# Weight loads moved from ScalarE's queue into SP's queue of x, one group ahead, in a ten-table embedding kernel

## The reference

```
embs    = [x_i @ w_i for i in 0..9]                 # x_i: 1024 x vocab_i, w_i: vocab_i x 64, float32
emb_sum = sum(embs)
q_emb   = sum((x_i ** 2) @ (w_i ** 2))
out     = concatenate([0.5 * (emb_sum ** 2 - q_emb)] + embs, axis=-1)
```

## Time and profile before

| | |
|---|---|
| median of 3 runs | 277.24 us (277.16 to 277.35) |
| profiled execution | 277.28 us |
| its span | 275.5 us |
| busy in the span | PE 214.9, DVE 222.2, ACT 225.6, POOL 117.5 us |
| moved by DMA | 113.92 MB, mean 413 GB/s |

### The profile page before, as it was taken

One profiled execution on the slowest core, in us unless ns is written; L12 is line 12 of the kernel. 1 busy time (PEld: TensorE's weight loads), 2 busy tenths in 40 slices (PEclk: granted clock), 3 DMA queues, 4 the chain that ended last, 5 costly groups with the idle time before them and its releaser, 6 DMA issues.

```text
span 275.5 us, 2719 instructions
## 1 busy us (share of the span) xinstructions
PE 214.9 (78%) x894; PEld 151.5 (55%) x894; DVE 222.2 (81%) x132; ACT 225.6 (82%) x272; POOL 117.5 (43%) x83
## 2 busy tenths in 40 slices
PE   0529889799988777878886887787688788698995
PEld 0416566576756555556664654554555555466752
DVE  2776876888798898878978978978987987999973
ACT  0648998999987788889868868868877887899984
POOL 0446667685414109257224134134045041083934
PEclk9977999999999999999999999999999999999999
DMA  7999999999999999999999999999999999999996
GB/s 257 436 412 431 419 424 414 427 425 426 421 425 425 421 426 421 422 426 427 421 432 422 426 423 424 423 426 430 418 426 428 421 431 425 407 420 415 410 396 231
DMA packets 15710, 113.92 MB, mean 413 GB/s; under 512 B 2000, under 2 KB 3280, under 8 KB 9168
## 3 DMA queue, kind: packets, MB, share of 16 engines
q1 hardware_dynamic: 11088, 106.96, 92.6%
q10 hardware_dynamic: 4608, 6.79, 6.7%
HBM read 110.85 MB, written 2.88 MB: 413 GB/s over the span
## 4 chain that ended last, share of the span: by engine, by line
DMA 71%; issue 13%; ACT 10%; PE 3%; POOLq 1%; POOL 1%; ACTq 1%; DVE 0%; SPq 0%
DMA x_ring<-in_x_dram 62%; DMA whole<-in_w_dram 8%; ACT is_set L380 7%; PE sums L518 2%; ACT turned L391 1%; ACT whole L372 1%; POOLq L197 1%; POOL is_one L498 1%; ACT results L396 1%; ACT L372 0%; ACTq L366 0%; ACT turned L440 0%; PE sums L573 0%; DVE is_one L614 0%; ACT odd_flag L443 0%
## 5 line engine op out<-in xcount | busy, mean ns | idle before, releaser
L614 DVE TENSOR_SCALAR_CACHE_REDUCE is_one<-x_ring 128x4096 uint8<-128x4096 f32 (+2 forms) x58 | 218.4, 3776 | 45.7 <-DMA x_ring<-in_x_dram 44.5
L380 ACT ACTIVATE is_set<-x_ring 128x2048 fp32r<-128x2048 uint32 (+2 forms) x106 | 190.1, 1796 | 32.1 <-DMA x_ring<-in_x_dram 31.7
L518 PE MATMUL sums<-is_set,low 128*128 128x512 f32 x396 | 133.0, 417 | 57.2 <-ACT is_set L380 42.5
L518 PE MATMUL sums<-is_set,high 128*128 128x512 f32 x396 | 125.2, 397 | 0.0
L518 PEld LDWEIGHTS sums<-is_set,low 128*128 128x128 f32 x396 | 68.3, 191 | 97.4 <-ACT is_set L380 42.7
L474 POOL CAST high<-whole 128x1024 fp32r<-128x1024 f32 (+5 forms) x31 | 27.1, 875 | 141.1 <-ACT whole L372 141.1
L518 PEld LDWEIGHTS sums<-is_set,high 128*128 128x128 f32 x396 | 75.5, 191 | 17.4
L476 POOL TENSOR_TENSOR low<-whole,high 128x1024 fp32r<-128x1024 f32 (+5 forms) x31 | 60.8, 1960 | 2.5
L372 ACT ACTIVATE whole<-whole 128x512 f32<-128x512 f32 (+5 forms) x31 | 16.5, 536 | 7.0 <-DMA whole<-in_w_dram 6.9
L380 ACT ACTIVATION_READ_ACCUMULATOR is_set<-x_ring 128x1 f32 x106 | 19.8, 186 | 0.0
L487 POOL TENSOR_TENSOR total<-total,turned 128x1024 f32<-128x1024 f32 x8 | 19.2, 2399 | 0.0
(11 more groups left out here) (38 smaller groups left out, 14.7 us busy)
## 6 DMA issues: line engine op xcount, KB each, us to landing
x_ring<-in_x_dram SPq DMA_DIRECT2D x42, 2048.0 KB, 21.3
x_ring<-in_x_dram SPq DMA_DIRECT2D x9, 1024.0 KB, 19.1
x_ring<-in_x_dram SPq DMA_DIRECT2D x11, 512.0 KB, 17.8
whole<-in_w_dram ACTq DMA_DIRECT2D x21, 256.0 KB, 9.7
out_dram<-results SPq DMA_DIRECT2D x9, 256.0 KB, 9.1
x_ring<-in_x_dram SPq DMA_DIRECT2D x4, 256.0 KB, 14.3
whole<-in_w_dram ACTq DMA_DIRECT2D x2, 192.0 KB, 7.2
whole<-in_w_dram ACTq DMA_DIRECT2D x4, 64.0 KB, 8.8
```

The source lines that it names most:

```text
L380: nc.scalar.activation(is_set[chunk.k % SETS][:, 0:length], in_ring(chunk.place, length).bitcast(U32), ACT.Sign, accum_out=set_counts[:, c ...
L518: last = nc.tensor.matmul(sums[:, summing(n, half), :], w, x[:, at:at + HALF], start=first, stop=False, skip_group_check=True)
L614: nc.vector.tensor_scalar(is_one[c % 2][:, 0:length], in_ring(at, length), 1.0, None, ALU.is_equal, ALU.add, accum_out=one_counts[:, c:c + ...
```

## The change

`AHEAD` becomes 2, and ScalarE issues no weights. SP does it between its loads of x: x load 0, then the weights of groups 0, 1 and 2, x load 1, and from there on the weights of group g+1 ahead of the first load of x of group g. The wait for `parts_ready` goes with them into SP's queue. `AHEAD` also sets when ScalarE squares (group g+1 after the third chunk of group g, where it was g+2) and when GpSimd adds a table's sums (one group after the copy, where it was two).

```
-AHEAD = 3
+AHEAD = 2
@@ plan_counts
         for load in own:
-            load.count = counts[-1]
+            load.count, load.group = counts[-1], one.group
@@ block.sync
-            free = 0
+            def load_w(group):
+                if group.g >= WHOLES:
+                    sp.wait_ge(parts_ready, group.g - WHOLES + 1)
+                at, n = group.tile * D, group.tiles
+                sp.dma_start(whole[group.whole][:, 0, 0:n, :], w_dram[group.table][:, at:at + n * D]
+                             ).then_inc(w_landed[group.whole], 16)
+
+            free, fetched = 0, 1
             for load in LOADS:
+                if load.i == 1:
+                    load_w(GROUPS[0])
+                while load.i > 0 and fetched < min(load.group.g + AHEAD, NGROUPS):
+                    load_w(GROUPS[fetched])
+                    fetched += 1
                 if load.free > free:
@@ block.scalar
-            def load_w(group):
...
-            for group in GROUPS[:AHEAD]:
-                load_w(group)
             act.wait_ge(constants, 8)
             for group in GROUPS[:AHEAD - 1]:
                 square(group)
             for group in GROUPS:
                 for c, chunk in enumerate(group.chunks):
                     count_set(chunk)
-                    if c == min(1, len(group.chunks) - 1):
-                        if group.g + AHEAD < NGROUPS:
-                            load_w(GROUPS[group.g + AHEAD])
                     if c == min(2, len(group.chunks) - 1) and group.g + AHEAD - 1 < NGROUPS:
                         square(GROUPS[group.g + AHEAD - 1])
```

## The result

| | before | after |
|---|---|---|
| median of 6 runs | 277.24 us (277.1 to 277.35) | 284.12 us (281.29 to 284.79) |
| ratio | | 1.0227 (95% interval 1.019 to 1.0264) |
| profiled execution, span | 277.28, 275.5 us | 284.56, 282.8 us |
| busy PE, DVE, ACT, POOL | 214.9, 222.2, 225.6, 117.5 us | 217.6, 222.5, 226.3, 117.5 us |

The kernel is slower, as forecast, but by 6.9 us where 3.9 were forecast, and the time lies outside the range of 279.9 to 283.0 us. Its runs also scatter over 3.5 us, where those of the kernel before agree within 0.25.

The account below looks back on a forecast made before the run. The prediction took the DMA stream of x plus a fixed tail to bound the kernel. Its terms, 0 + 0 + 3.9 + 0 + 0, on 277.24 gave 281.1 us, with a range of 279.9 to 283.0 us.

Parts of the forecast that it names:

- a stream and a fixed tail: Whole kernel: x in transfer without a hole until 267.0 us, then some 6.7 us of small work on the last tile.
- SP's added issues: SP's queue: 31 more issues, 10 to 14 us against 210 us of waiting, counted at 0.
- ScalarE's freed ones: ScalarE: 31 issues, 10.4 us, go; nothing waits for its queue while the stream is full, counted at 0.
- The first wait: Start of SP's queue: the weights of group 3 wait for group 0's split, with x behind; a hole of 3.9 us.
- The end: Last group squared after chunk 97 instead of 93; weighing ends 0.7 us before GpSimd's last masks, so hidden, counted at 0.
- The wait of w8: SP's queue: group 8's weights hold back x load 9 until group 5 is split; margin -0.2 to +1.2 us, counted 0.
- a second hole at w8: Rival: group 5 ready 1 to 3 us later adds 0.5 to 2.5 us, 281.6 to 283.6; 0.22 together with the end.
- No change: Rival: who issues makes no difference, if group 3's weights find x still in transfer; 277.2 us, chance 0.03.
- faster: Rival: one queue runs the DMA engines better than two in turns, at 436 GB/s some 276.2 us; chance 0.05.

Follow-up runs that it names:

- e6: Changed kernel with five buffers of weights instead of three and three of parts instead of four, same order in SP's queue; 277.07 us.
- e12: Changed kernel run a third time as it is, for its spread; 281.93 us, ratio 1.0155 to the kernel before.
- e0: Changed kernel run again as it is, for a trace with another time; 281.71 us, ratio 1.0149 to the kernel before.
- e3: Changed kernel with only the square of group 5 moved, to after chunk 5 as in the kernel before; 281.01 us.
- e5: Changed kernel with the product of the low part left out in chunks 3 to 7 (tables 4 and 7); 281.74 us.
- e8: Changed kernel with each product of chunks 3 to 7 (tables 4 and 7) made twice; 286.10 us.
- e1: Changed kernel with ScalarE issuing the weights of groups 3 to 5 where the kernel before did, SP all others; 278.60 us.
- e9: Changed kernel with the weights of group g+1 behind the last load of x of group g, except the last three groups; 277.22 us.

## Why the prediction was wrong

**What held.** That the kernel is a stream and a fixed tail: the tail stayed at 6.7 us, and spans differ by their holes and by the lag of the last part, a term that the prediction did not have. SP's added issues cost nothing and ScalarE's freed ones gave nothing that shows (e6 has both and full slices; its 0.5 us under the kernel before has no cause shown). The first wait: 3.9 us forecast, 3.8 to 4.0 us in every trace of the changed kernel. Here two small misses cancelled. w3 was issued at 8.97 us and not at 9.28, but the stream ran again in effect from 10.66 us, worked out from the 568 KB of the stretch 10 to 12 us at 425 GB/s. That is 1.7 us after the issue, where 1.4 was taken between bounds of 1.0 and 1.9. The first packet of w3 started 0.95 us after its issue. The Trainium skill's 0.6 us to the first byte ("DMA: Bandwidth & Descriptors", Specifications), by which the prediction made the hole 3.1 us, is shorter than the trace's time; the hole of 3.8 us goes with the trace. The end was covered, as worked out: the weighing ends at 272.8 us, the masks start at 273.9. The lowest run of each of the three sets, 281.13 to 281.29 us, is the forecast of 281.1, one hole and no more.

**The step that failed** is "The wait of w8", counted at 0: "ScalarE needed from 22.08 us (chunk 3) to 35.2 us (end of chunk 7), 13.1 us almost without a gap", so it "can start there. Chunk 7 ends at 32.7 us". I took a stretch in which ScalarE was busy for one in which ScalarE alone sets the pace. Before, TensorE did chunk 3 and what follows at the high clock. In the profile after it did chunks 3 and 4 at 1.2 GHz, and ScalarE stood 3.27 us at its copy until TensorE was through with chunk 5. Load 3 also landed at 20.0 to 20.5 us where 19.5 was forecast. In place of 0 the term measured 3.0 us in the first profile, 2.9 in e12, 0.6 in e0, and 0.0 once the square was early (e3). In e0 and e5 w8 went out at 37.4 to 37.7 us, against 36.9 forecast, and 0.6 and 1.0 us were lost without an empty stretch; whether the late w8 made the stream slow there was not shown.

**The rival** "a second hole at w8" was named at 281.6 to 283.6 us, with a chance of 0.22 for it and the end together. It is the case that came. Its own rule fits, too: group 5 was ready 3.8 us later than worked out, and the hole was 3.0 us. But it allowed for a delay of 1 to 3 us only, and the median lies 0.5 us above its 283.6. The range ended at 283.0 and so took in 1.4 of the rival's 2.0 us, which is not "nearly all" of it. The clock that goes with it was not in my working, although the trace of the kernel before has TensorE at 1.2 GHz from 17.3 to 24.1 us. "No change" and "faster" are out: the wait ended too late for the one, and for the other the rate in mid kernel did not move.

**Chance in the number.** Of the six runs of the first set four fell among the long ones with a low mean clock; in each of the two later sets it was two of six. The median of all 18 runs is 282.4 us, inside the range. So the size of the miss is in part luck, but the forecast of no second hole is not saved by that, since 8 of 18 runs took over 283 us.

**What stays open.** Why the clock is low in other stretches from run to run of the same kernel, and so why the first set of runs has a median of 284.12 us and the next two 281.7 and 281.9. That TensorE's time sets the second hole rests on e8's times and on the copy's wait in the traces (3.27, 1.13, 0.42 and 4.05 us); that the clock is what stretches it is read from the traces and the mean clocks, as no run set the clock itself. It is also open whether the first hole helps to bring about the second. In the profile after TensorE stood idle for 3.3 us from 19.3 us, until chunk 3 was ready, and its clock fell at 21.5; in e0 it stood idle for 2.3 us from 14.1 us and 1.6 us from 20.5 us, and the clock fell at 16.0 and 22.9. But e1, without the first hole, has a second one of 2.4 us. What decides which of the 16 DMA engines falls behind, and by how much, wasn't tried.

## What to carry to other kernels

A wait in the queue that feeds a stream costs whatever it outlasts the transfers ahead of it: put it where enough bytes stand ahead (e9), or give it more buffers, so that it has long been met (e6, five for three). Check this first at the start, where nothing is in flight and short groups come one after the other. When a due time is worked out along one engine that looks busy, work it out along the slowest engine that feeds it too, at its lower clock: a forecast of 0 with 1 us of margin there is a range, not a zero.

## What was not expected of the hardware

The 16 parts of one load can land 2 to 4 us apart for most of a kernel, and the end waits for the last: 2.2 us before, with the last but one 0.2 us ahead of it; 3.8 us in e0, with one part 1.7 us behind all others. Two things went with it. Some packets are slow: those of 16 KB take 0.61 us as a rule, but after the second hole of the profile after ten took 1.0 to 1.6 us between 42.4 and 43.1 us. A hole isn't needed for that: in e5, whose stream was not empty there, 21 took 0.9 to 1.9 us between 39 and 44 us, while e3, with an early w8, had none from 30 to 50 us. And instruction fetches travel on these engines too: a 16 KB fetch took 1.07 us at 74.4 us of e0, a packet that started at 75.5 us, as it ended, took 1.11 us instead of 0.61, and the lag grew from 2.4 to 3.9 us between two landings there. In the kernel before a fetch of 1.13 us at 43.9 us stands between the landings where the lag grew from 0.6 to 1.6 us. Other fetches changed nothing: the one at 72.6 us left it at 1.8. Whether fetch, slow packet and last part are on the same engine the trace as read here doesn't tell.

The clock of TensorE differs between runs of one kernel. It was low from about 22 to 31 us in the profile after, and in e0 from about 16 to 19 and from 23 to 26 us. The mean over a run parts the long runs from the short ones, as shown above, but it doesn't order the long ones: the profile after has 0.976 with 284.56 us, e0 0.970 with 283.19. What counts is where it is low. The column doesn't show all of it either: the first pairs of products, from 9.7 to 15 us of the profile after, took 1.05 us each while it stands at 1.00.
